# First batch convolved by the raw taps on x·W_in, the product of both weights formed behind it

## The reference

```python
xz = x @ W_in                              # W_in: 256 x 512
xc, r = split(xz)                          # 256 channels each
xs = causal_conv(xc, conv_w) + conv_b      # conv_w: 256 x 256 x 4 taps, full mixing of channels
u = silu(xs)
dbc = u @ W_x                              # dt (128), B (16), C (16)
delta = softplus(dbc[:, :128] @ W_dt + b_dt)
h = exp(delta * A) * h + (delta * u) * B   # scan over 512 tokens, 16 states per channel
y = sum_n h * C + u * D
out = (y * silu(r)) @ W_out + xs           # then layernorm(x + out), and the second block
```

## Time and profile before

| | us |
|---|---|
| median of 3 runs | 491.65 (489.69 to 491.72) |
| the profiled execution | 488.78 |
| its span, first to last instruction | 487.0 |
| mean granted TensorE clock | 0.943 of full |

### The profile page before, as it was taken

One profiled execution on the slowest core, in us unless ns is written; L12 is line 12 of the kernel. 1 busy time (PEld: TensorE's weight loads), 2 busy tenths in 40 slices (PEclk: granted clock), 3 DMA queues, 4 the chain that ended last, 5 costly groups with the idle time before them and its releaser, 6 DMA issues.

```text
span 487.0 us, 6491 instructions
## 1 busy us (share of the span) xinstructions
PE 413.7 (85%) x2021; PEld 249.4 (51%) x2021; DVE 313.9 (64%) x624; ACT 294.4 (60%) x628; POOL 284.9 (59%) x261
## 2 busy tenths in 40 slices
PE   5989898899999799899875789866968998999991
PEld 3433353444445344446333346342755777888881
DVE  0302664588665579973689967999489396544355
ACT  4255588994786993676795376971252465553152
POOL 2010086678987889777889769996562253331012
PEclk9999999999999979999989699977997899999996
DMA  7102501106101004111002204870400000000013
GB/s 235 44 0 72 148 23 31 34 2 160 59 24 42 23 0 93 64 43 42 7 18 67 89 25 157 250 282 0 174 0 1 2 0 1 3 0 1 1 44 129
DMA packets 18709, 29.10 MB, mean 60 GB/s; under 512 B 2698, under 2 KB 10676, under 8 KB 18420
## 3 DMA queue, kind: packets, MB, share of 16 engines
q1 hardware_dynamic: 18676, 28.70, 19.1%
HBM read 22.27 MB, written 2.23 MB: 50 GB/s over the span
## 4 chain that ended last, share of the span: by engine, by line
PE 45%; ACT 15%; DVE 12%; POOL 8%; issue 8%; POOLq 0%; DVEq 0%; ACTq 0%
PE bank L538 8%; PE bank L554 7%; ACT loop_buf L1027 6%; ACT front_a L1037 5%; PE bank L675 4%; POOL state L1565 3%; PE bank L851 3%; PE bank L827 3%; PE bank L619 2%; PE bank L641 2%; DVE state L1186 2%; PE bank L859 1%; PE bank L576 1%; PE bank L798 1%; PE bank L818 1%
## 5 line engine op out<-in xcount | busy, mean ns | idle before, releaser
L1186 DVE TENSOR_TENSOR_SCAN state<-front_a,bank 128x512 f32<-128x512 f32 x88 | 102.6, 1204 | 42.9 <-PE bank L538 21.3
L538 PEld LDWEIGHTS bank<-ident,loop_buf 128*128 128x128 f32 x512 | 60.4, 146 | 83.5 <-issue 40.1
L538 PE MATMUL bank<-ident,loop_buf 128*128 128x128 f32 x512 | 84.8, 290 | 17.2 <-ACT loop_buf L1027 15.4
L1037 ACT ACTIVATE front_a<-loop_buf,a_neg 128x512 f32<-128x512 f32 x128 | 84.4, 713 | 7.9 <-DVE copy L1186 4.8
L1027 ACT ACTIVATE loop_buf<-copy,b_rows 128x256 f32<-128x256 f32 x190 | 78.9, 496 | 0.1
L554 PE MATMUL bank<-front_c,conv_raw 128*128 128x512 f32 x128 | 60.7, 607 | 2.5 <-ACT front_c L902 0.9
L1186 DVE TENSOR_TENSOR_SCAN copy<-front_a,bank 128x512 f32<-128x512 f32 x40 | 47.1, 1207 | 23.8 <-PE bank L538 8.4
L1565 POOL TENSOR_TENSOR state<-state,front_a 128x1024 f32<-128x1024 f32 x22 | 52.2, 2375 | 9.0 <-DVE state L1186 9.0
L1565 POOL TENSOR_TENSOR state<-state,c_own 128x1024 f32<-128x1024 f32 x22 | 51.9, 2361 | 9.2 <-DVE state L1186 9.0
L675 PE MATMUL bank<-state,fold 128*64 128x512 f32 x176 | 50.7, 656 | 1.5 <-POOL state L1565 1.5
L1578 POOL TENSOR_TENSOR loop_buf<-copy,b_rows 128x512 f32<-128x512 f32 x31 | 33.4, 1079 | 24.4 <-ACT copy L902 21.9
(11 more groups left out here) (205 smaller groups left out, 745.9 us busy)
## 6 DMA issues: line engine op xcount, KB each, us to landing
front_a<-c_stage SPq DMA_DIRECT2D x32, 128.0 KB, 2.9
c_own<-c_stage SPq DMA_DIRECT2D x32, 128.0 KB, 2.8
loop_buf<-front_b SPq DMA_DIRECT2D x32, 128.0 KB, 2.3
copy<-in_L_attn_x SPq DMA_DIRECT2D x4, 512.0 KB, 3.8
front_b<-in_L_ffn_wo SPq DMA_DIRECT2D x1, 2048.0 KB, 10.0
copy<-in_L_ffn_wq SPq DMA_DIRECT2D x1, 2048.0 KB, 8.3
out<-loop_buf SPq DMA_DIRECT2D x3, 512.0 KB, 3.0
conv_raw<-in_L_attn_conv_w SPq DMA_DIRECT2D x2, 512.0 KB, 3.8
```

The lines of the kernel that those rows point to most:

```text
L538: return pe.transpose(dst, src, ident[:])
L1037: act.activation(decay[:, u % NDA, :], delta_wide[:, b % 2, k, :], ACT.Exp, scale=a_neg[:, k, m:m + 1]).then_inc(decay_made, 1)
L1186: dve.tensor_tensor_scan(state[t % NH][:, j, :], decay[:, u % NDA, :], bank[BU_BANK[u % NBU]][:], 0.0, ALU.mult, ALU.add).then_inc(scanned, 1)
```

## The change

Batch 0 no longer waits for the product of the weights. x is loaded first. PE turns x, turns the raw taps (`cw`), projects x by the left half of W_in (`xc0`, `xc1`, two 128x512 matmuls each, copied by ACT to `xcT`, padded by 3 zero columns), and convolves `xcT` with `conv_t`. The turning of W_in and the product (`wT`, `vc0` to `vc3`) come as pieces of `FIRST_FRONT` behind `s1`, around `s3`. `cw`, `xc` and `vc` get fixed PSUM banks. `r0`, `r1` of batch 0 come behind `du1`; ACT copies them only after `make_decay(1)`. Of batch 1 only `xT0`, `xT1` stay ahead of the loop; its eight quarters come two a step at t = 0, 1, 2 and 3 (`FIRST_CONV`). The condition of `widen_c(0)` is kept in words, and `vc3` is now filled at its new place.

```diff
+FIRST_FRONT = ("xT0", "xT1", "cw0", "cw1", "cw2", "cw3", "xc0", "xc1", "vec", "cv0a", "cv0b", "cv0c", "cv0d", "cv1a",
+               "cv1b", "cv1c", "cv1d", "su", "dt", "bc", "cr", "dl0", "dl1", "rs", "s1", "wT", "vc0", "vc1", "s3",
+               "vc2", "vc3", "du0", "du1")
+SECOND_FRONT = ("r0", "r1")
+EARLY = ("xT0", "xT1")
+FIRST_CONV = {"cv0a": -16, "cv0b": -16, "cv0c": -15, "cv0d": -15, "cv1a": -14, "cv1b": -14, "cv1c": -13, "cv1d": -13}
+HEAD_BANK = {"cw0": 0, "cw1": 2, "cw2": 3, "cw3": 4, "xc0": 5, "xc1": 1, "vc0": 0, "vc1": 2, "vc2": 3, "vc3": 1}
...
-        late = {"cv1b": -16, "cv1c": -15, "cv1d": -14}
...
-                if b * NST + (late.get(piece, off) if b == 1 else off) == t and not (b == 1 and piece in EARLY)]
+                if b * NST + (FIRST_CONV.get(piece, off) if b == 1 else off) == t and not (b == 1 and piece in EARLY)]
...
+        xcT = front_b[:, 0:KD * (PAD + L)].rearrange("p (k l) -> p k l", k=KD)
...
+            load_x(0)
             for k in range(KD):
                 load(f"conv{k}", conv_raw[:, k, :], conv_w[k * P:(k + 1) * P].rearrange("p i t -> p (i t)"))
             load("w_in", w_in_s, W_in.rearrange("(k p) n -> p k n", p=P))
-            load_x(0)
...
                 if g == 0:
-                    wait_filled(sp, ("vc", 3))
+                    wait_filled(sp, ("vc3", 0))
...
                     if b == 0:
-                        wait_drained(pe, ("vc", 2 * i + k // 2))
-                    mm = pe.matmul(at(name)[:], conv_x[:, k, i, o * P:(o + 1) * P], xT[:, i, k:k + L],
+                        wait_drained(pe, (f"cw{2 * o + k // 2}", 0))
+                        wait_drained(pe, (f"xc{i}", 0))
+                    elif b == 1:
+                        wait_drained(pe, (f"vc{2 * i + k // 2}", 0))
+                    taps, rows = (conv_t, xcT) if b == 0 else (conv_x, xT)
+                    mm = pe.matmul(at(name)[:], taps[:, k, i, o * P:(o + 1) * P], rows[:, i, k:k + L],
                                    start=(j == 0), stop=(j == TAPS * KD - 1))
...
+                elif piece[:2] == "xc":
+                    pe.wait_ge(in_w["w_in"], 16)
+                    wait_drained(pe, ("xT0", b))
+                    wait_drained(pe, ("xT1", b))
+                    for k in range(KD):
+                        mm = pe.matmul(t[:], w_in_s[:, k, o * P:(o + 1) * P], xT[:, k, PAD:],
+                                       start=(k == 0), stop=(k == KD - 1))
...
+            front(0, "r0")
+            turn_bu(0)
+            turn_bu(1)
+            front(0, "r1")
             for piece in EARLY:
                 front(1, piece)
-                if piece == "cv0b":
-                    front(0, "du0")
-                    front(0, "du1")
-                elif piece in FIRST_BU:
-                    turn_bu(FIRST_BU.index(piece))
...
             for piece in FIRST_FRONT:
-                if piece == "s3":
-                    front(1, "xT0")
-                    front(1, "xT1")
                 front(0, piece)
-            front(0, "du0")
-            front(0, "du1")
             make_z(0, 0)
             make_z(0, 1)
             act.wait_ge(a_ready, 2)
             make_decay(0)
             make_decay(1)
-            front(1, "cv0d")
+            for piece in SECOND_FRONT:
+                front(0, piece)
+            for piece in EARLY:
+                front(1, piece)
...
+            pool.memset(xcT[:, :, 0:PAD], 0.0).then_inc(conv_pad, 1)
```

More of the change, by code:

```diff
@@ L131, in add_pieces @@
                     held[0] = None
+            elif piece in HEAD_BANK:
+                fills.add((piece, b), HEAD_BANK[piece])
             elif piece not in NO_FILL:
                 add_rest((piece, b))
[L135 to L140, removed]
     NPAIR = NST // 2
@@ L150, in fronts @@
     def fronts(t):
[L153 removed]
         return [(b, piece) for b in range(B - 1, 0, -1) for off in sorted(FRONT_AT) for piece in FRONT_AT[off]
[L155 removed]
+                if b * NST + (FIRST_CONV.get(piece, off) if b == 1 else off) == t and not (b == 1 and piece in EARLY)]
     def norms(t):
         return NORM_AT.get(t - (B - 1) * NST)
[L161 to L166 removed]
+    add_pieces(0, FIRST_FRONT + SECOND_FRONT)
+    add_pieces(1, EARLY)
     for t in range(B * NST):
@@ L557, in convolve @@
                     fill_done(name, mm)
+            raw_taps = conv_raw[:].rearrange("p o (i t) -> p o i t", t=TAPS)
             def front(b, piece):
@@ L567, in front @@
                 t = at(name)
-                if piece in ("xT0", "xT1"):
+                if piece[:2] == "cw":
+                    o, k0 = o // 2, 2 * (o % 2)
+                    pe.wait_ge(in_w[f"conv{o}"], 16)
+                    for k in range(2):
+                        for i in range(KD):
+                            a = (k * KD + i) * P
+                            mm = turn(t[:, a:a + P], raw_taps[:, o, i * P:(i + 1) * P, k0 + k])
+                elif piece[:2] == "xc":
[5 more added lines that the diff above has]
+                                       start=(k == 0), stop=(k == KD - 1))
+                elif piece == "wT":
+                    for i in range(KD):
+                        for j in range(KD):
+                            a = i * DM + j * P
+                            mm = turn(t[:, a:a + P], w_in_s[:, j, i * P:(i + 1) * P])
+                elif piece == "vec":
+                    pe.wait_ge(in_w["vec"], 16 * 8)
+                    mm = pe.transpose(t[:, 0:NVEC], vec_rows[:], ident[0:NVEC, 0:NVEC])
+                elif piece[:2] == "vc":
+                    wait_drained(pe, ("wT", 0))
+                    j, k = o // 2, 2 * (o % 2)
+                    for i in range(KD):
+                        mm = pe.matmul(t[:].rearrange("p (t o) -> p t o", t=2), w_inT[:, i, j * P:(j + 1) * P],
+                                       conv_t[:, k:k + 2, i, :], start=(i == 0), stop=(i == KD - 1))
+                elif piece in ("xT0", "xT1"):
                     pe.wait_ge(in_x[b % 2], 16 * (b // 2 + 1))
@@ L711, in make_v @@
                 fill_done(("v", v), mm)
[L714 to L744, removed]
             for piece in FIRST_FRONT:
@@ L925, in front @@
                     if b == 0 and o == 0:
-                        wait_drained(act, "vec")
+                        wait_drained(act, ("vec", 0))
                     if b >= 1:
```

36 lines of the change are left out of this document (29 added, 7 removed).

## The result

| | before | after |
|---|---|---|
| median | 490.85 us (6 runs, 489.69 to 493.05) | 503.94 us (6 runs, 501.35 to 507.57) |
| the profiled execution, its span | 488.78, 487.0 | 504.56, 502.8 |
| mean granted TensorE clock | 0.943 | 0.931 |

The ratio is 1.027, 95% interval 1.022 to 1.032: slower by 13.1 us at the medians. The two profiled executions lie 15.8 us apart. The interval is wide because executions of the changed kernel themselves differ by 6 us.

What follows compares the result with a forecast made beforehand. A serial head up to the first scan, then PE pacing the loop, bound the kernel. A 10.6 us shift at the table plus 3.5 for clock drops, 14.1, on the median 491.65 gave 505.7; predicted 505.5, range 499 to 510.

Steps and rivals of the forecast that it cites:

- The head, 13.3: On PE ahead of the first convolution: it starts at 13.3 instead of 19.42, saving about 6.2 us.
- The product filled at 48.5: On PE behind s1: ACT's copy of turned W_in, then 7.11 us of product, fill `vc3` at 48.5.
- The queue behind the product, first decay 60.2: On SP: C loads, then delta transfers, wait for `vc3`; first decay at 60.2, 2.5 us later than before.
- The quarters, 4.31 us a step: In the PE-paced loop: steps 0 to 2 hold two quarters each and take 4.31 us instead of 2.6.
- The granted clock, two new falls, 3.5: Behind new PE idles ahead of `vc0` and batch 1's x: one clock drop each, 1.8 + 1.7 = 3.5 us.
- The shift at the table, 10.6 + 3.5 = 14.1: At ACT's silu table of batch 1: 10.6 us later at full clock, 3.5 for clock drops, reaching the end.
- the 63.4 of the sum: PE's loop start: at about 63.4, after ACT's copies of r0, r1 free the banks at 62.8.
- the rival of overlapping transfers: C loads and delta transfers on SP overlap: decay at 56.1, 10.6 becomes 6.5, total 498 to 501.7; chance 0.08.
- the estimate of 4.8 us for both batches: C loads and delta transfers together, by the skill's 435 GB/s ceiling within SBUF: an estimate of 4.8 us.
- full clock: PE's new idles cost nothing, or the drop at dt goes too: +8.8 to +10.6, 500.5 to 502.3; chance 0.18.
- The swallowed loop: The loop hides the five moved quarters, only the late start counts: +2.5 to +4, 494 to 495.7; chance 0.05.
- gave the time back: Later stages, mostly after slice 20, leave the lower clock: at most some 27 us regained, 488 or less; chance 0.03.

Runs made afterwards that it cites:

- Experiment 1: Also `delta_first`: the changed kernel with SP issuing batch 0's delta transfers ahead of the C loads; 496.48 us, ratio 1.0105.
- Experiment 2: Also `quarters_back`: the changed kernel with batch 1's first five quarters back ahead of the loop and ACT's r, x copies ahead of the first decay; 496.46 us.
- both_back: The changed kernel with delta transfers ahead of the C loads and the five quarters back ahead of the loop; 496.28 us, ratio 1.0111.
- Experiment 3: Also `no_idle`: the changed kernel with ten unread matmuls, three before the product and seven before batch 1's x; 499.61 us, ratio 1.0166.
- experiment 6: Also `four_delta_loads`: the changed kernel with eight delta transfers of 128 KB made four of 256 KB; 503.33 us, ratio 1.0254.
- experiments 2 and 4: The second of these: the kernel before with only batch 1's five quarters moved into the loop, two a step in steps 0 to 3; 500.14 us, ratio 1.0174.
- moved_no_idle: The kernel before with batch 1's five quarters moved into the loop and five unread matmuls in their old place; 499.35 us, ratio 1.0161.

## Why the prediction was right

The forecast was +14.1 and 505.5 us; the medians give +13.1 and 503.94, the profiled executions +15.8. The path was the forecast one, place for place. That the total came out within 1 us of the median is in part luck: up to the table the clock cost 1.2 us less than the forecast had, and small pieces that it had too short cost 0.9 more.

- **The head, 13.3**: 13.44 measured. Loading x first cost nothing but the 0.18 us.
- **The product filled at 48.5**: the first C load went out at 48.88. It is the right place by two errors that cancel. I had the fall to 1.2 GHz ahead of dt stay and left the one ahead of the product out of that number; in fact dt ran at full clock (-1.7) and the product did not (+1.7, 8.80 against 7.11).
- **The queue behind the product, first decay 60.2**: 60.75. Experiment 1 shows it: with SP's order alone turned round, the decay is at 54.94 and 7.5 us of the 13.1 are gone.
- **The quarters, 4.31 us a step**: in the timeline the second and third steps' turnings stand at 70.79 and 75.10, 4.31 apart. Experiment 2 shows that their place costs; `both_back` shows that it is not a sum with the first: each alone gives back 7.5 us, both together 7.7.
- **The granted clock, two new falls, 3.5**: both came. Experiment 3 gave back 3.7 in the trace with a head 0.3 later, so 4.0, and 4.3 at the medians. But the sum had the two on top of the old fall at dt, and that one vanished, which stood only among the rivals. So up to the table the clock made a net of 4.0 - 1.7 = 2.3 and not 3.5. The fall at the loop was sized from two quarters alone, 1.7; it covered the first step's turning too, and cost 2.3.
- **The shift at the table, 10.6 + 3.5 = 14.1**: 13.85, and the same at the scan of step 5. With the measured net of the clock it would be 10.6 + 2.3 = 12.9. The other 0.9 us are small pieces: at full clock PE's loop would start 0.2 later than the 63.4 of the sum (62.20 in `no_idle`, whose product is done 1.4 earlier), step 0 takes 0.5 more between turning and quarters (62.20 to 63.56 there, instead of 0.87), and step 3 takes 0.4 more, while the 0.2 that the sum gave to ACT before step 3 was not needed.
- **The end**: a third fall, at 96 us, not in the forecast, added 1.6 us.

What the prediction had wrong did not decide it: against the rival of overlapping transfers it argued that SP's 0.6 us for each issue sets the pace. For the delta transfers that is not so: experiment 6 halves the issues and nothing moves, and the other argument given there, a DMA share near 0.99, is the one that counts. For the C loads it may well be so: the engines were 0.53 busy while SP issued them. No run took the C loads apart, so why these took their 5 us stays argued. What is measured is that the two batches moved at 191 and 215 GB/s, and not at the 397 of the first loads, and so took the one's time and then the other's. The Trainium skill, "DMA: Bandwidth & Descriptors", section "Where 436 GB/s comes from", gives 435 GB/s as the ceiling within SBUF. It bears on the delta transfers alone, since the C loads start in HBM, which the estimate of 4.8 us for both batches passed over. The delta transfers ran at about half of it, 215 to 223 GB/s, and the measured rate decides.

The rivals: full clock did not come true, since 4 us were shown to hang on the new falls, though its second half, no fall at dt, did. The swallowed loop fell with experiments 2 and 4. No stage after the head gave the time back: the table loads at 138.30, 216.06 and 447.44 of the kernel before stand at 153.76, 231.01 and 463.24, +15.5, +15.0 and +15.8.

## What to carry to other kernels

A piece moved past others takes with it every wait that names it: look on each in-order queue, the DMA issuer's too, for a wait on the moved piece, and list what stands behind it; here 6 us saved on PE became 3 lost on the first scan through one line on SP that nobody had moved. Work that fills an engine's idle is free only there: the same quarters made each step 1.72 us longer in a loop that this engine paces, and where they left, the clock fell behind the new idle as well. Two faults on one path do not add: mending either gave 7.5 us, mending both 7.7. Put the deferred work into the waits that the critical chain already has: so placed, and with delta ahead of C on SP, the idea gave 0.5%.

## What the runs showed of the hardware that I had not expected

- Ten useless matmuls made the kernel 4.3 us faster (503.9 to 499.6), by keeping 2.4 GHz through two waits.
- Waits of one length came out differently: behind the 1.96 us ahead of dt the clock fell in the kernel before and in `four_delta_loads` (3.65 and 3.59 us for dt), for a part of dt in `both_back` (2.90), and not in the changed kernel, `delta_first`, `quarters_back` or `no_idle` (1.95 to 1.96). The product behind the same 3.14 us took 7.11 in `four_delta_loads`, 8.80 in the changed kernel and 10.13 in `delta_first`. So the same list of instructions can end some us apart.
- Eight transfers of 128 KB and four of 256 KB, 1 MB from on-chip memory to on-chip memory either way, took the same 6.9 to 7.1 us from first issue to the engine that waited.
- In the profiled execution of `moved_no_idle` the first product took 8.95 us instead of 7.11 while the clock column showed 1.00 from 10 to 20 us; what slowed it stays open.
